# Attention exponentials taken by query and turned on TensorE, with the turned banks copied by ScalarE and VectorE, in a two-layer kernel

## The reference

```python
q = (x @ wq).reshape(Bq, Tq, N_KV, N_REP, HEAD_DIM)      # 2 kv heads, 4 queries each
k_lat = (x @ wk_down).reshape(Bq, Tq, N_KV, D_LAT)       # 32 latent columns a head
v_lat = (x @ wv_down).reshape(Bq, Tq, N_KV, D_LAT)
k = jnp.einsum('bkhl,ld->bkhd', k_lat, wk_up)
v = jnp.einsum('bkhl,ld->bkhd', v_lat, wv_up)
scores = jnp.einsum('bqhrd,bkhd->bhrqk', q, k) * scale
scores = jnp.where(causal, scores, jnp.finfo(scores.dtype).min)
probs = jax.nn.softmax(scores, axis=-1)
y = jnp.einsum('bhrqk,bkhd->bqhrd', probs, v)
return y.reshape(Bq, Tq, N_HEADS * HEAD_DIM) @ wo
```

## Time and profile before

| | |
|---|---|
| three runs, us | 1813.36, 1815.53, 1820.96 (median 1815.53) |
| the profiled execution, us | 1823.07 |
| its span, us | 1821.3 |
| mean granted clock of PE | 0.945 of 2.4 GHz |
| busy: PE, DVE, ACT, POOL | 88%, 80%, 61%, 41% of the span |
| chain that ended last | PE 58%, issue 11%, DVE 7%, POOL 6%, ACT 4%, DMA 3% |

### The profile page before, as it was taken

The page is one execution under the profiler, slowest core; times in us unless marked ns, Lnnn a source line. Parts: engine busy times, 40 slices in busy tenths (PEclk is TensorE's granted clock), DMA queues, the critical chain, the costliest instruction groups (busy, mean ns, idle before and its releaser), DMA issues.

```text
span 1821.3 us, 24301 instructions
## 1 busy us (share of the span) xinstructions
PE 1609.8 (88%) x8311; PEld 773.9 (42%) x8352; DVE 1460.3 (80%) x2032; ACT 1106.2 (61%) x1551; POOL 750.6 (41%) x603
## 2 busy tenths in 40 slices
PE   4444588989999999999999999999999999899888
PEld 1221134444454445444544445444544445345545
DVE  3799799889998998889988989889998999721514
ACT  3535387568756876667756875678746873542141
POOL 0455354444634454435534453535534553401002
PEclk8665699999999999999999999999999999899999
...
GB/s 215 205 239 238 258 214 232 207 194 199 218 125 187 192 233 145 202 170 210 188 154 186 198 232 122 213 169 228 181 172 184 190 236 123 117 1 0 1 7 6
DMA packets 107886, 309.18 MB, mean 170 GB/s; under 512 B 15970, under 2 KB 32244, under 8 KB 107764
## 3 DMA queue, kind: packets, MB, share of 16 engines
...
## 4 chain that ended last, share of the span: by engine, by line
PE 58%; issue 11%; DVE 7%; POOL 6%; ACT 4%; DMA 3%; POOLq 0%; DVEq 0%; ACTq 0%
PE ps_pair L726 16%; PE ps_pair L880 8%; PE ps_pair L824 7%; PE ps_pair L811 7%; POOL sb_hc L1555 6%; PE ps_pair L900 5%; PE ps_pair L842 4%; PE ps_y L662 4%; DMA sb_ring<-spread_dram 3%; DVE sb_hst L1281 2%; PE ps_pair L680 2%; PE ps_pair L825 1%; DVE sb_nmax L1422 1%; PE ps_pair L828 1%; PE ps_pair L791 1%
## 5 line engine op out<-in xcount | busy, mean ns | idle before, releaser
L1555 POOL TENSOR_TENSOR sb_hc<-sb_hst,sb_crep 128x512 f32<-128x512 f32 x512 | 653.8, 1280 | 848.7 <-DVE sb_hst L1281 739.8
L1281 DVE TENSOR_TENSOR_SCAN sb_hst<-sb_ring,ps_in 128x512 f32<-128x512 f32 x512 | 620.5, 1212 | 26.9 <-ACT sb_ring L969 23.6
L969 ACT ACTIVATE sb_ring<-sb_ring,sb_A 128x512 f32<-128x512 f32 x512 | 347.2, 714 | 196.3 <-DMA sb_ring<-spread_dram 187.6
L1273 DVE TENSOR_TENSOR ps_in<-sb_ring,ps_brow 128x512 f32<-128x512 f32 x512 | 354.9, 693 | 28.3 <-DMA sb_ring<-spread_dram 15.3
L946 ACT ACT_TABLE_LOAD x227 | 291.2, 1283 | 16.5 <-issue 5.3
L880 PE MATMUL ps_pair<-sb_mix,sb_ew 128*128 128x512 f32 x512 | 250.2, 621 | 9.9 <-ACT sb_g L1093 4.2
L662 PE MATMUL ps_y<-sb_hc,sb_const 128*32 128x512 f32 x1024 | 146.0, 655 | 58.6 <-POOL sb_hc L1555 49.4
L824 PE MATMUL ps_pair<-sb_g,sb_h 128*128 128x512 f32 x320 | 171.5, 618 | 4.4 <-ACT sb_sq L1115 2.4
L811 PE MATMUL ps_pair<-sb_h,sb_g 128*128 128x512 f32 (+3 forms) x512 | 164.4, 451 | 7.2 <-DVE sb_nmax L1422 2.8
L880 PEld LDWEIGHTS ps_pair<-sb_mix,sb_ew 128*128 128x128 f32 x512 | 95.9, 197 | 143.6 <-issue 104.4
L900 PEld LDWEIGHTS ps_pair<-sb_ew,sb_eh 128*128 128x128 f32 x1024 | 120.7, 192 | 20.8 <-issue 16.4
...
## 6 DMA issues: line engine op xcount, KB each, us to landing
sb_ring<-spread_dram SPq DMA_DIRECT2D x512, 512.0 KB, 6.1
...
```

The costliest lines, as they stand in the source:

```text
L969: act.activation(ring[:, n % RING, 0, :], ring[:, n % RING, 0, :], ACT.Exp, scale=A[d][:, g:g + 1]).then_inc(sem["dA"], 1)
L1273: dve.tensor_tensor(ps_in[n % 2][:], ring[:, n % RING, 1, :], ps_brow[:], ALU.mult).then_inc(sem["dbu"], 1)
L1281: dve.tensor_tensor_scan(hst[:, HST_SLOT[n], :], ring[:, n % RING, 0, :], ps_in[n % 2][:], 0.0, ALU.mult, ALU.add).then_inc(sem["scan"], 1)
L1555: pool.tensor_tensor(hc[:, n % HC, :], hst[:, HST_SLOT[n], :], crep[n // NU][:], ALU.mult).then_inc(sem["hc"], 1)
```

## The change

The order of the attention is now by kv head. `scores(i)` makes the scores of two query heads of one kv head for one tile. After DVE's maximum ACT takes the exponential straight from the score bank, with the maximum as bias, into `pexp[t]`, queries on the partitions (two instructions per step). A bank pair is thus free only when ACT is done (`pexp`), no longer after the maximum (`smax`). After the eight steps of a kv head come its five rounds: `turn(i)` turns four 128x128 blocks of exponentials per bank on PE, ACT copies the first bank of a round (`ptr`) and DVE the second (`ptd`) to `pT`, and `values` uses the copies. The second product of the scores, `pick`, the split maxima and `mT` are gone. `pexp` and `pT` lie in tiles of the experts (mix, ea, eh) and in res, sq and g1; ACT's wait for the previous output (`outn`) and for the experts' last bank stands before the first exponential, as before. The 13 early loads have a semaphore of their own, `w_early`, for which PE and DVE wait before the first turned weight; DVE waits for the other 13 before the last h2 weight. `fwb2`, `cb`, `fwnc`, `finc` and the centring of `ffw2` move there. All order strings are new (one line of one is shown).

```diff
-    qT=2, kT=4, kz=1, vlat=1, smax=16, split=2, mT=1, pexp=20, rz=2, yT=2,
+    qT=2, kT=4, kz=1, vlat=1, smax=16, pexp=16, ptr=10, ptd=10, rz=2, yT=2,
 ...
+QUERIES = (0, 1, 3, 2)
+MAXIMA = KV * TT * REP // 2
 
 
 def maximum(i):
 
-    return i // (2 * REP), i // 2 % REP, i % 2
+    return i // (2 * TT), QUERIES[i // 2 % TT], i % 2
 ...
-    uses += [[(f"s{i}", "smax", i + 1)] for i in range(MAXIMA)] + [[("mT", "mT", 1)]]
-    for i in range(len(ROUNDS) + 1):
-        uses += [[(f"r{i}_{hf}", "pexp", 2 * i + hf + 1) for hf in range(2)] if i < len(ROUNDS) else []]
-        if i % LAST == 1:
-            uses[-1] += [(f"att{i // LAST}", "yT", i // LAST + 1)]
+    for k in range(KV):
+        uses += [[(f"s{i}", "pexp", i + 1)] for i in range(k * MAXIMA // KV, (k + 1) * MAXIMA // KV)]
+        for i in range(k * LAST, (k + 1) * LAST):
+            uses += [[(f"r{i}_0", "ptr", i + 1), (f"r{i}_1", "ptd", i + 1)]]
+            if i % LAST == 1:
+                uses[-1] += [(f"att{k}", "yT", k + 1)]
+        uses += [[]]
 ...
-HOLD = dict(mo0="var1", mo1="var1", mo2="var2", mo3="var3", att0="ao", att1="ao")
+HOLD = dict(mo0="var1", mo1="var1", mo2="var2", mo3="var3", att0="s8", att1="ao")
 ...
 ORDER = dict(
     PE=(
-        "xxxxxxuxrxxruxrxhrurhxrhruxxrrhrruxhrrrxhrxhuuhrrhrrxuurxxxrxhxhxurrxhrrrrrrrurrxrrrrrrrhruhhhrhhxrrurrrrrurrr"
+        "xxxxxxxxuxrruxrxhrrhxrurhhxrxrrrxhruhurxrrxhrruhuxrrxrxxxhrhxuurhxrxhrurrrrxrrrrrrrrrururrhhrhrhhurrxrrrhrrrrru"
 ...
-        pexp = [mix[:, 0:2, :], mix[:, 2:4, :], g1[:, 2:4, :]]
+        rows = [eh[:, 1, 0:1, :], eh[:, 0, :, :], ea[:, 0:3, :], mix[:]]
+        pexp = [rows[t].rearrange("p a b -> p (a b)").rearrange("p (r n) -> p r n", r=REP) for t in range(TT)]
+        pT = [[eh[:, 1, 1, :], ea[:, 3, :]], [g1[:, 2, :], g1[:, 3, :]], [res[:], sq[:]]]
 ...
                 for dst, src in later[:EARLY]:
-                    sp.dma_start(dst, src).then_inc(w_later, 16)
+                    sp.dma_start(dst, src).then_inc(w_early, 16)
 ...
                 def scores(i):
-                    tl, r, hf = maximum(i)
-                    t = TILES[hf][tl]
+                    k, t, half = maximum(i)
+                    hf = 0 if t in TILES[0] else 1
                     claim(f"s{i}")
                     if i == 0:
                         pe.wait_ge(sem["qT"], row("qT", 2))
                         pe.wait_ge(sem["kT"], row("kT", 4))
-                    for k in range(KV):
-                        pe.matmul(ps_pair[i % 2][:, k, 0:(t + 1) * P], qT[:, tl, r, :], kz[:, 2 * k + hf, 0:(t + 1) * P],
-                                  start=True, stop=False)
-                    for k in range(KV):
-                        ins = pe.matmul(ps_pair[i % 2][:, k, t * P:(t + 1) * P], identb[:], maskb[:], start=False, stop=True)
+                    for s in range(2):
+                        pe.matmul(ps_pair[i % 2][:, s, 0:(t + 1) * P], qT[:, TILES[hf].index(t), 2 * half + s, :],
+                                  kz[:, 2 * k + hf, 0:(t + 1) * P], start=True, stop=False)
+                    for s in range(2):
+                        ins = pe.matmul(ps_pair[i % 2][:, s, t * P:(t + 1) * P], identb[:], maskb[:], start=False, stop=True)
                     done(ins)
 
-                def turned_scores(i):
+                def turn(i):
                     k, units = ROUNDS[i]
                     for hf, (t, j) in enumerate(units):
                         o = claim(f"r{i}_{hf}")
-                        if i == 0 and hf == 0:
-                            pe.wait_ge(sem["mT"], row("mT", 1))
-                        tl = TILES[hf].index(t)
-                        pe.matmul(o[:], kz[:, 2 * k + hf, j * P:(j + 1) * P], qT[:, tl, :, :], start=True, stop=False)
-                        ins = pe.matmul(o[:], pick[:, 2 * k + hf:2 * k + hf + 1].broadcast_to([P, P]), mT[:, tl, :, :],
-                                        start=False, stop=(j < t))
-                        if j == t:
-                            ins = pe.matmul(o[:], maskb[:], identb[:].unsqueeze(1).broadcast_to([P, REP, P]),
-                                            start=False, stop=True)
+                        pe.wait_ge(sem["pexp"], row("pexp", 2 * (TT * k + QUERIES.index(t)) + 2))
+                        for r in range(REP):
+                            ins = pe.transpose(o[:, r * P:(r + 1) * P], pexp[t][:, r, j * P:(j + 1) * P], ident)
                         done(ins)
 
                 def values(i):
@@ -835,31 +832,26 @@
                     if i % LAST == 0:
                         claim(f"att{k}")
                         pe.wait_ge(sem["vlat"], row("vlat", 1))
-                    pe.wait_ge(sem["pexp"], row("pexp", 2 * i + 2))
+                    pe.wait_ge(sem["ptr"], row("ptr", i + 1))
+                    pe.wait_ge(sem["ptd"], row("ptd", i + 1))
                     for hf, (t, j) in enumerate(units):
                         for into, w in ((ps_att, vlat[:, j, k * LAT:(k + 1) * LAT]), (ps_z, ones[:])):
                             for r in range(REP):
                                 ins = pe.matmul(into[LAT * r:LAT * (r + 1), t * P:(t + 1) * P], w,
-                                                pexp[i % 3][:, hf, r * P:(r + 1) * P],
+                                                pT[i % 3][hf][:, r * P:(r + 1) * P],
                                                 start=(i % LAST == 0 and hf == 0), stop=(i % LAST == LAST - 1 and hf == 1))
                     ins.then_inc(sem["att"], 1)
 
-                for i in range(MAXIMA):
-                    scores(i)
-                    yield
-                o = claim("mT").bitcast(BF16).rearrange("p (t r n) -> p t r n", t=2, r=REP)
-                pe.wait_ge(sem["split"], row("split", 2))
-                for tl in range(2):
-                    for r in range(REP):
-                        ins = pe.transpose(o[:, tl, r, :], nsplit[:, tl, r, :, :].rearrange("p g c -> p (g c)"), identb[:])
-                done(ins)
-                yield
-                for i in range(len(ROUNDS) + 1):
-                    if i < len(ROUNDS):
-                        turned_scores(i)
-                    if i >= 1:
-                        values(i - 1)
-                    yield
+                for k in range(KV):
+                    for i in range(k * MAXIMA // KV, (k + 1) * MAXIMA // KV):
+                        scores(i)
+                        yield
+                    for i in range(k * LAST, (k + 1) * LAST + 1):
+                        if i < (k + 1) * LAST:
+                            turn(i)
+                        if i > k * LAST:
+                            values(i - 1)
+                        yield
                 pe.wait_ge(sem["yT"], row("yT", 2))
 ...
-                for _ in range(MAXIMA):
-                    yield
-                act.activation(mT, full("mT").bitcast(BF16).rearrange("p (t r n) -> p t r n", t=2, r=REP), ACT.Copy
-                               ).then_inc(sem["mT"], 1)
-                yield
-                for i in range(len(ROUNDS) + 1):
-                    if i < len(ROUNDS):
+                for k in range(KV):
+                    for i in range(k * MAXIMA // KV, (k + 1) * MAXIMA // KV):
+                        _, t, half = maximum(i)
                         table(EXP_LN)
                         if i == 0:
                             act.wait_ge(sem["outn"], row("outn", 0))
                             act.wait_ge(sem["full_e"], row("full_e", 0))
+                        act.wait_ge(sem["smax"], row("smax", i + 1))
+                        for r in (2 * half, 2 * half + 1):
+                            ins = act.activation(pexp[t][:, r, :], ps_pair[i % 2][:, r % 2, 0:(t + 1) * P], ACT.Exp,
+                                                 bias=nmax[:, k, t, r:r + 1])
+                        ins.then_inc(sem["pexp"], 1)
+                        yield
+                    for i in range(k * LAST, (k + 1) * LAST):
                         if i >= 3:
                             act.wait_ge(sem["att"], row("att", i - 2))
-                        for hf in range(2):
-                            act.activation(pexp[i % 3][:, hf, :], full(f"r{i}_{hf}")[:], ACT.Exp).then_inc(sem["pexp"], 1)
-                    if i in (LAST, 2 * LAST):
-                        k = i // LAST - 1
-                        table(EXP_LN)
-                        act.wait_ge(sem["att"], row("att", i))
-                        act.wait_ge(sem["yT"], row("yT", k))
-                        act.activation(rz[:], ps_z[:], ACT.Ln).then_inc(sem["lnz"], 1)
-                        act.wait_ge(sem["lnz"], row("lnz", k + 1))
-                        act.activation(rz[:], rz[:], ACT.Exp, scale=-1.0).then_inc(sem["rz"], 1)
+                        act.activation(pT[i % 3][0], full(f"r{i}_0")[:], ACT.Copy).then_inc(sem["ptr"], 1)
+                        yield
+                    table(EXP_LN)
```

(26 more changed lines are left out.)

111 lines of the change are left out of this document (42 added, 69 removed).

## The result

The changed kernel takes 1835.1 us in the median of four runs (1831.45 to 1839.37), the kernel before 1816.9 in four: a ratio of 1.0096, interval 1.0074 to 1.0119. It is **slower by 1%**; 1807.5 was forecast. The profiled execution took 1831.45 us, the fastest of its four, while that of before (1823.07) was the slowest of its own; the traces therefore show 8.4 us of a difference of 18. One later run of the kernel before (5694 us) and one of e11 (1850 us, mean granted clock 0.908) fell far out of line and stay out of every ratio here.

The account below looks back on a forecast made before the run. PE was taken to limit both parts of a body stage, DVE close behind. Stage 0 -2, stage 1 -2, body 0, stage 7 0, flush -4 sum to -8, from the median 1815.5 to 1807.5 us; range 1773 to 1840.

Parts of the forecast that it names:

- first part 126.7 - 1 = 125.7: Body stage, x3 to s0: PE's work unchanged and still the limit, 1 us less because DVE has three units less there.
- rival (c): Rounds of transposes and values run at 1.2 GHz: about +8 us per stage over seven stages, 1863 us; chance 0.05.
- the body's own terms: Body stage: first part 125.7, s0 0.5, DVE's attention work 73.7, stalls 1.5; together 201.4 against 201.1, rounded to 0.
- halfway point: DVE stalls of 6 us per body stage: the sum is +22, 1838 us.
- rival (b): Exponentials in the score bank's cycle, behind scan exponentials, delay DVE's maxima: +8 per body stage, +47 in all, 1862; chance 0.20.
- The attention part changes its limit from PE to DVE: Body stage, s0 to x3: DVE's work 73.7 us, PE's about 53.5, so PE's saving cannot be used.
- DVE's stalls, taken as 1.5: Attention part of a body stage: DVE's stalls go from 9.7 us to 1.5 in the new order.
- 3 us of stall per body stage: The DVE stall in a body stage from which the slower case, exponentials in the bank's cycle, was to decide.
- Stage 7: Between s0 and x3 DVE's work comes to 77.6 us against the window's 77.7: change 0.
- Flush: Attention with no units interleaved: rounds, masks and split maxima save time, part is given back; -4 net, bounds -9 and +3.
- what is given back: Flush losses: bank pair's cycle +6, rounds filling and draining +4, first head's open work +2, wait for previous output +2.5.
- Stages 0 and 1: Split weight wait: stage 0 gains 2 of DVE's 9.1 us wait, DMA 98% busy; stage 1 gains 2.

Follow-up runs that it names:

- e11: e1 with ACT's scan decays of units 38 to 63 cut to 128 of 512 columns, part of the work left out; its profiled execution took 1814.2 us.
- e1: The changed kernel with extra f32 products in PE's idle time at the end of the attention; 1818.8 us, ratio to before 1.000.
- e8: The kernel before with the same extra products in PE's idle time at the end of the attention as e1; 1810.1 us, ratio 0.996.
- e10: e1 with drive and scan of units 38 to 63 cut to 128 of 512 columns, part of the scan left out; two runs, 1785.3 and 1796.7 us.
- e12: e1 with the score banks handed back one by one, each by its own exponential; 1806.1 us, ratio 0.994.

## Why the prediction was wrong

**The failed step** is in the body: "first part 126.7 - 1 = 125.7", with the words that PE's work is unchanged there. The work was, the clock was not: the first part took 128.7. e1 has 126.1 with the clock held, so 2.6 us a stage, 13 over the body, were missing for the clock, a term that the sum did not have. That the rest came out to 0.4 us is in part luck: the 126.7 that it starts from holds falls of the clock itself (e8: 124.9 without them), and the 1 us that was to go did not. The mechanism was named as rival (c) with a chance of 0.05, but in the wrong place: it looked for the fall in the rounds of transposes, where the clock stayed at 1.00 (965 to 977 us in the body stage above), and took its evidence against from the attention part of before. The trace of before had the right place on show: it too fell to 1.2 GHz at three seams, and the earlier trace rows gives 0.99 for first parts. A change that gives DVE more unit steps between the links of the closing chain has to be read against that.

The forecast was 27.6 us too low. The traces account for 16.4 of it: 15.7 in the five first parts, 5.8 in stage 7, less 4.2 in the flush, 1.3 ahead of the body and 1.0 in the attention parts, plus the 1.5 that the body's own terms (201.4 against 201.1, five times) gave and that was set to 0. The other 11 are the step from one trace to the median: the 7.5 us by which the profiled execution of before was slow were taken off, and that of the changed kernel was its fastest, 3.7 us below its median. The 1835.1 lies inside the range of 1773 to 1840 and near the 1838 of the halfway point of rival (b); that is luck, since the price of (b) was put together from other causes.

**Right for a wrong reason: the attention part.** 73 to 77 was forecast and 75.5 measured, with DVE busy 70.8 (73.7 forecast). "The attention part changes its limit from PE to DVE" is false: e10 took 27 us from DVE for 2.2. What holds it is PE's own work in line with its waits, of which the ring product, maximum, two exponentials, free bank is one that e12 shows (2.0 us). PE was to have 53.5 us of work there and had 58.6: one more `reduce` fell into the part (L665, 8.1 us busy against 6.3), and the 80 transposes are busy for 11.3 us, not 8.8, where the chain leaves gaps between them. In the flush, with nothing interleaved, the 15 us came out (63.0 to 48.1). DVE's stalls, taken as 1.5, were 4.8, of which 2.7 are maxima that wait for score products (2.4 before). The point "3 us of stall per body stage", from which rival (b) was to decide, was thus passed, and e12 shows its cycle. Its price was too high (+8 a stage against +1.1). ACT's 187.6 us wait behind the DMA plays next to no part here: 2.2 us of it fall into this attention part, and e11 shows that shorter decays bring nothing.

**Stage 7**: 0 forecast, +5.8. With the clock held its first part is 121.7 against 120.3, from 125.1; the attention stays at 77 to 84 in all versions that leave no work out (before 77.8, changed 78.7). It was not taken further apart.

**Flush**: -4 forecast, -8.2 in the traces. The round is 2.03 us (2.0 forecast), PE timeline of the changed kernel against the earlier trace rows:

```profile
1759.45 0.66 PE L826 MATMUL ps_pair<-sb_const,sb_mix 128*128 128x128 f32 x4
1759.94 0.60 PE L826 MATMUL ps_pair<-sb_const,sb_ea 128*128 128x128 f32 x4
...
1761.48 0.66 PE L826 MATMUL ps_pair<-sb_const,sb_mix 128*128 128x128 f32 x4
```

Four transposes take 0.49 us there, 0.44 forecast; the 14.5 us laid to what is given back were some 4 too many.

**Stages 0 and 1**: -4 forecast, -5.3 in the traces, within their scatter; the whole times don't bear out the part laid to the split wait.

What stays open: 10 of the 18 us between the medians lie outside the two traces. Single runs of either kernel differ by 8 us, and I can't say where the other runs spent theirs.
